# A recurrence loop in which TensorE makes two products ahead of a turn's sums and ScalarE copies one of them a turn later

## What is computed

```python
x = rmsnorm(resid) * norm_w
skip = x @ skip_w.T                       # 512 channels
x = silu(conv4(x @ in_w.T) + conv_b)      # this is u
delta = softplus(x @ Wd1.T @ Wd2_w.T + Wd2_b)
Bm, Cm = x @ WB.T, x @ WC.T               # with x @ Wd1.T: the product "db"
h = exp(delta * A) * h + (delta * x) * Bm # per token, 512 channels x 16 states
y = (sum(h * Cm) + x * W_D) * silu(skip)
y = y @ out_w.T
```

## Time and profile before

| what | value |
|---|---|
| median of 3 runs | 1883.05 us (1880.05 to 1884.74) |
| the profiled execution's own time | 1880.88 us |
| its span (first to last instruction) | 1879.1 us |
| busy in the span: PE, DVE, POOL, ACT | 1625.9, 1452.1, 1241.9, 1137.6 us |
| mean granted TensorE clock | 0.943 of full speed |

### The profile page before, as it was taken

How to read it: one execution, slowest core, us unless ns; L and a number is a source line. 1 busy time by engine, 2 the same in 40 slices (tenths; PEclk the granted TensorE clock), 3 DMA queues, 4 the chain that set the end, 5 groups by cost and what they waited for, 6 DMA issues and landing times. The chain is left out here.

```text
span 1879.1 us, 32964 instructions
## 1 busy us (share of the span) xinstructions
PE 1625.9 (87%) x9680; PEld 1053.9 (56%) x9681; DVE 1452.1 (77%) x2270; ACT 1137.6 (61%) x2662; POOL 1241.9 (66%) x920
## 2 busy tenths in 40 slices
PE   8788888787888878884589999998999999999997
PEld 5455544454555544552256666665776555555686
DVE  6899999999999999999758888887533444444488
ACT  5778888888888888886335555564322333333325
POOL 2999999999999999999556888873401333333300
PEclk9899999999998899996679999999999999999999
DMA  8645455544454554445247755542264222222272
GB/s 234 145 105 125 113 135 136 124 109 104 103 127 113 136 136 117 110 100 120 77 114 170 197 183 159 152 143 74 81 234 157 85 85 85 87 86 84 72 269 90
DMA packets 179286, 238.30 MB, mean 127 GB/s; under 512 B 24714, under 2 KB 115725, under 8 KB 177070
## 3 DMA queue, kind: packets, MB, share of 16 engines
q1 hardware_dynamic: 160606, 200.64, 41.2%
q0 software_dynamic: 9888, 27.80, 4.2%
q10 hardware_dynamic: 8656, 8.18, 1.6%
HBM read 172.15 MB, written 65.90 MB: 127 GB/s over the span
## 5 line engine op out<-in xcount | busy, mean ns | idle before, releaser
L760 DVE TENSOR_TENSOR_SCAN ps_h<-ps_h,inject 128x1024 f32<-128x1024 f32 x160 | 365.4, 2284 | 27.7 <-ACT ps_h L589 27.4
L376 POOL TENSOR_TENSOR inject<-common,bc_n 128x2048 f32<-128x2048 f32 x63 | 285.5, 4544 | 60.7 <-issue 60.7
L376 POOL TENSOR_TENSOR inject<-dx_n,bc_n 128x2048 f32<-128x2048 f32 x64 | 290.4, 4551 | 0.0
L1537 ACT ACTIVATE expT<-ps_t 128x512 f32<-128x512 f32 x256 | 147.1, 593 | 164.5 <-PE ps_t L2042 164.4
L589 ACT ACTIVATE ps_h<-common,a_neg 128x256 f32<-128x256 f32 x512 | 211.4, 462 | 44.3 <-DVE hc L773 33.1
L760 DVE TENSOR_TENSOR_SCAN h_pool<-ps_h,inject 128x1024 f32<-128x1024 f32 x96 | 218.9, 2281 | 15.4 <-ACT ps_h L589 12.3
L589 ACT ACTIVATE ps_h<-delta_n,a_neg 128x256 f32<-128x256 f32 x512 | 212.7, 461 | 27.5 <-DVE hc L773 22.9
L1690 DVE TENSOR_REDUCE neg_max<-ps_s 128x2 f32<-128x512 f32 x256 | 173.4, 682 | 71.6 <-PE ps_s L2031 70.9
L385 POOL TENSOR_TENSOR h_pool<-h_pool,bc_n 128x1024 f32<-128x1024 f32 x96 | 227.0, 2365 | 0.0
L2696 PE MATMUL ps_uh<-arena,s_xT 128*128 x440 | 210.1, 600 | 4.7 <-issue 4.6
L2400 POOL DMA_INDIRECT token_results<-common,e_y_row x82 | 80.1, 976 | 190.6 <-DVE common L2549 190.6
(11 more groups left out here) (344 smaller groups left out, 3610.6 us busy)
## 6 DMA issues: line engine op xcount, KB each, us to landing
common<-dup_rows SPq DMA_DIRECT2D x120, 256.0 KB, 5.8
bc_n<-bc_rows SPq DMA_DIRECT2D x64, 256.0 KB, 4.7
delta_n<-dup_rows SPq DMA_DIRECT2D x64, 256.0 KB, 4.3
dx_n<-dup_rows SPq DMA_DIRECT2D x64, 256.0 KB, 7.4
arena<-slot_rows SPq DMA_DIRECT2D x110, 136.0 KB, 2.1
arena<-token_results SPq DMA_DIRECT2D x8, 1536.0 KB, 18.6
dup_rows<-delta SPq DMA_DIRECT2D x32, 256.0 KB, 3.6
dup_rows<-dx SPq DMA_DIRECT2D x32, 256.0 KB, 3.8
```

What stands on the lines that cost most here:

```text
L376: nc.gpsimd.tensor_tensor(inject[:, at:at + 2, :, :], dx_n[c // 2][:, None, :, c % 2, :].to_broadcast([P, 2, JB, L]), bc_n[b % 2][:, 0, nq ...
L760: nc.vector.tensor_tensor_scan(out.rearrange("p j t -> p (j t)"), ps_h[k % 2][:, :, :].rearrange("p j t -> p (j t)"), inject[:, k % RING, ...
L1537: nc.scalar.activation(expT[:, h % (2 * HG), :, :], ps_t[h % 2][:, :, :], ACT.Exp).then_inc(h_exp, 1)
```

## The change

Three calls are moved; nothing is added or removed.

```diff
@@ ScalarE, turn loop
-                if entry and i in (14, 15):
-                    take_skip(b + 2, i - 14)
+                if entry and i == 14:
+                    take_skip(b + 2, 0)
+                if front and tail and i == 0:
+                    take_skip(b + 1, 1)
@@ TensorE, turn loop
                 if tail and i == 2:
                     project_out(b - 1)
+                if front and i == 4:
+                    project_db(b + 1)
+                if entry and i == 14:
+                    project_skip(b + 2, 1)
                 sums(b, i)
...
-                if front and i == 4:
-                    project_db(b + 1)
...
-                if entry and i in (13, 14):
-                    project_skip(b + 2, i - 13)
+                if entry and i == 13:
+                    project_skip(b + 2, 0)
```

## The result

| | before | the change |
|---|---|---|
| median | 1881.97 us (4 runs, 1880.05 to 1884.74) | 1859.74 us (4 runs, 1854.71 to 1861.99) |
| profiled execution: span | 1879.1 us | 1858.4 us |
| rounds 1 to 14 | 753.16 us | 734.81 us |
| round 0 | 57.86 us | 53.98 us |

The ratio is 0.9877, with a 95% interval of 0.9853 to 0.9901: the change is 1.2% faster. The forecast was 1862.5, within 1857 to 1872. So the number came out. The experiments show that its terms, read as what each move gives, did not: the two skip moves, to which the forecast gave 15.3 of its 19.4 us, make the kernel slower when they are made without the move of db.

The account below looks back on a forecast made before the run. DVE was taken to bound rounds 1 to 14, with POOL close behind. The terms 10.6 + 4.7 + 1.7 + 2.45 = 19.4 us gave 1861.5 to 1863.7, stated as 1862.5 us, range 1857 to 1872.

Parts of the forecast that it names:

- the place of the remaining wait: Turn 5, where the decay follows silus on ACT: DVE's waits at `ps_h` should stay near 18 us.
- the later copy being free: Copy of the second skip half between the decays of turns 2 and 3: takes 0.60 us, costs ACT nothing.
- POOL's margin at the scan of turn 2: POOL's second inject serves turns 2 and 3 at 431.26, the scan wants it at 431.69: 0.43 us.
- 10.6 + 4.7: DVE's turn-2 waits at `h_pool` for ACT, 10.6 us, and the excess of turn-5 waits, 4.7 us, both gone.
- 1.7 + 2.45: From db ahead of turn 4's sums: DVE's waits at dx, 1.7 us, and its wait in round 0, 2.45 us.
- had little to lose in such a round: Behind ACT's 1.63 us wait in `take_db`, DVE's next idleness in round 6 was only 0.44 us, at dx.
- the check beside it: If rounds 1 to 14 all take round 2's 52.35 us, they give back 20.3 us, with round 0 22.7.
- POOL's inject: Rival, chance 0.16: in turn 2 DVE waits for POOL's inject instead; 8 us of the gain lost, 1870 us.
- The larger sum: Rival, chance 0.08: more than the sum is gained, 22.7 us over rounds 0 to 14, giving 1859 us.
- the wait moves to silus: Rival, chance 0.07: late `ps_a` convolutions make turn 5 pay what turn 2 saved; 15 of 19.4 lost, 1878 us.
- The clock was given 0.04: Rival, chance 0.04: TensorE at 1.2 GHz from 427 to 441, too late for db and silus; 1955 us at the extreme.
- The clock rule: TensorE throttles after idleness, sustained work lifts it; shorter idleness ahead of turn 14's sums keeps full clock, sum stays 19.4 us.

Follow-up runs that it names:

- the padding: Full change plus two small thrown-away GpSimd products ahead of each round's first inject, from round 1 on; ratio 1.0000 to the kernel before.

## Why the prediction was right, and where it was not

**Right:** the ratio, the place of the remaining wait (turn 5, 18.3 us, behind silus; shown by shortening silus), the vanished wait of turn 2 and of `take_skip`, the later copy being free (with db and the product early, 0.9887 without it against 0.9877 and 0.9891 with it), PE's idleness in turn 14 falling from 3.7 to 2.0 us, POOL's margin at the scan of turn 2 (0.43 forecast; 0.3 in round 7, 0.5 in the mean, 0.4 to 0.5 by the padding), and rounds of 52.3.

**Wrong: what each move is worth.** The forecast gave the two skip moves 10.6 + 4.7 us by themselves and db 1.7 + 2.45. Measured by themselves, the skip moves cost about 15 us and db gives 11 (5.4 in its trace). Put on top of the skip moves, db is worth 0.8 + 1.2 = 2.0%, some 38 us. The step that failed is the sentence that behind `take_db` DVE "had little to lose in such a round", with the check beside it. It took rounds 6 and 2 as a picture of rounds without idleness in turn 2. But in those rounds PE still had the second skip product to make between turn 14 and turn 4. The skip moves take it out of there. PE then comes to the sums of turn 4 about 2 us earlier, POOL's product does not, and PE waits 3 us for it. db, behind that sum, starts no earlier, and in eleven of 14 rounds it runs wholly or in part at 1.2 GHz (in round 12 of that run the granted clock over db's 3.73 us was 0.50). The clock's part is shown: with added matmuls in that gap the loss of 0.8% went (0.9981, interval up to 1.0000). The part of the order is shown by the full change: with db ahead of the sum, ACT's wait of 51.5 us in `take_db` is 0.7.

So the total was right because all moves were in it: db ahead closes just the hole that the skip moves open. The forecast did not see this hole. It put db in for 1.7 + 2.45 us and for another reason, so that the hole stayed closed is luck and not its reasoning. With db in place the skip moves, 10.6 + 4.7 = 15.3 us in the sum, measured 9 us in the timed runs and 16.2 in the traces. The sum was right for the three moves together, and wrong as an account of separate gains.

**Missed in the profile before.** DVE's idleness in turn 2 came with the low clock, and not with the order alone. In the trace before, the second skip product takes 2.85 to 3.78 us in nine of the rounds 1 to 14, and these are exactly the nine with a wait in turn 2; in the five others it takes 1.99, and there is none. PE had idled 2.1 to 4.0 us ahead of it in the nine, and 0.2 to 3.3 in the five. The waits of DVE, 0.3 to 1.9 us, are of the size of what the slow product takes more, 0.9 to 1.8. This is read from the rows; no run removed the clock's drop there and left the order as it was.

**The terms, by size.** Rounds 1 to 14 gave 18.35 for 10.6 + 4.7 + 1.7 = 17.0. Round 0 gave 3.88 for 2.45; its later small waits, which the sum left out, went as well. The first scan was 1.25 late, which no step had; it starts between 47.5 and 49.1 us in the traces of all these kernels, so this looks like the spread of executions and not like the change. The rounds gave back 22.2 us, nearer to the 22.7 of the check by round 2's time than to the 19.4 of the sum.

**The rivals.** POOL's inject did not take the place of the wait, but by 0.5 us in the mean only. In round 2 it ended 0.09 us ahead of the scan, and with the padding 0.09 us is also what lies between the two when the scan does wait for it. And when it is made to take it, the whole gain goes; its price was too low: by the forecast's way 1.38 us of lateness costs 13 us, and it cost 22. The larger sum, 1859 with a chance of 0.08, is nearer to the measured 1859.74 than the forecast; 1859.74 lies at the edge of the sum's own range, 1859 to 1867. That the wait moves to silus is what the later copy does alone. The clock was given 0.04 as a danger between 427 and 441; it was a real one in another place, where PE idles ahead of the sums of turn 4, and the change is what avoids it. Its price has a slip: 7.1 x 14 is 99 and not 95, which makes the extreme some 1962.

**The clock rule.** After the shorter idleness the clock stayed full, as the rule had it that the forecast takes from the Trainium skill: in 13 of 14 rounds the convolutions that now follow POOL's sum run at full pace, after waits of at most 1.7 us. In round 7, after 2.00 us, they don't. The rows before are as mixed: waits of 3.26 and 3.10 us without a drop (rounds 2 and 5), one of 2.13 with it (round 13, below). So the trace agrees with the rule's direction and gives no bound.

```profile
751.60 0.93 PE L941 MATMUL ps_y<-h_pool,sel 128*32 128x256 f32 x8 [2.13 <-POOL h_pool L385]
752.46 3.34 PE L865 MATMUL ps_a<-xnT,w_skip 128*128 128x256 f32 x8
```

The forecast weighed it for the convolutions and not for the gap that the skip moves open elsewhere.

## What to carry to other kernels

These are rules drawn from this one kernel. Taking work out of a stretch of TensorE only helps what follows if nothing in that stretch waits for a later engine; else the time turns into idleness there, and what stands behind it may run at half clock. Price a removed wait by going on to the next place where the late engine's result is needed, with that engine no earlier, and don't borrow the price from stretches that happen to have no such wait. Work that doesn't need the late engine's result goes ahead of work that does in every in-order queue at once; moved in one place only, the wait moves to the next and may meet a lower clock there.

## What the runs showed of the hardware

**A scan with both inputs in SBUF beside GpSimd.** The scan of 128x1024 takes 2.26 to 2.30 us with its decay in PSUM, whatever GpSimd does. With its decay in SBUF it took 3.99 in the mean of rounds 1 to 14: 2.92 to 3.95 in thirteen of them and 9.61 in round 5. GpSimd was busy over the whole of each of the thirteen, so how long such a scan takes alone is not shown.

In the thirteen rounds GpSimd paid as well: its product beside the scan took 4.3 us instead of 2.4. Round 6, with the scan first:

```profile
391.63 3.66 DVE L774 TENSOR_TENSOR_SCAN ps_h<-zln,inject 128x1024 f32<-128x1024 f32 x1
```

```profile
388.58 4.54 POOL L379 TENSOR_TENSOR inject<-common,bc_n 128x2048 f32<-128x2048 f32 x1
393.10 4.33 POOL L388 TENSOR_TENSOR h_pool<-h_pool,bc_n 128x1024 f32<-128x1024 f32 x1
```

The times fit with the two taking turns: the scan ends at 395.29, 2.2 us after the inject (393.12), and the product at 397.43, 2.1 us after the scan.

In round 5 the scan lost every turn. GpSimd's work, of two SBUF inputs, ran back to back until 340.8 with its usual 2.40 and 4.57 us, the scan ended 2.2 us after it, and the next inject then waited for the scan:

```profile
333.37 9.61 DVE L774 TENSOR_TENSOR_SCAN ps_h<-zln,inject 128x1024 f32<-128x1024 f32 x1
```

```profile
333.95 2.40 POOL L388 TENSOR_TENSOR h_pool<-h_pool,bc_n 128x1024 f32<-128x1024 f32 x1
336.26 4.57 POOL L379 TENSOR_TENSOR inject<-dx_n,bc_n 128x2048 f32<-128x2048 f32 x1
343.06 4.52 POOL L379 TENSOR_TENSOR inject<-dx_n,bc_n 128x2048 f32<-128x2048 f32 x1 [2.23 <-DVE ps_h L774]
```

The Trainium skill (SBUF — State Buffer, Who interferes with whom) says that a VectorE instruction with two SBUF inputs contends with a GpSimd instruction that reads SBUF, and one with a single SBUF input does not. By that rule the trace agrees on both sides: 2.28 against 3.99 us. Of VectorE's two-port modes the Trainium skill also says there that whoever issues first holds the ports for the whole instruction and the other fully blocks. The thirteen rounds look like such turns of whole instructions. In round 5 the scan had begun 0.58 us before GpSimd's product and was held all the same; what decides who goes first stays open.

**Idle TensorE, slower TensorE.** A db product of 1.97 us took up to 3.73 after 3 us of idleness (granted clock 0.50), and 1.97 again (granted clock 1.00) when four needless matmuls filled part of it.
